# A segment softmax on one core: the scan carries the preceding edges' maximum, ScalarE clamps, VectorE scales edge rows

## The reference

```python
q = (x @ qw + qb).reshape(N, HEADS, CH)
k = (x @ kw + kb).reshape(N, HEADS, CH)
v = (x @ vw + vb).reshape(N, HEADS, CH)
alpha = jnp.sum(q[dst] * k[src], axis=-1) * SCALE
m = jax.ops.segment_max(alpha, dst, num_segments=N)
a = jnp.exp(alpha - m[dst])
denom = jax.ops.segment_sum(a, dst, num_segments=N)
a = a / denom[dst]
msg = v[src] * a[:, :, None]
out = jax.ops.segment_sum(msg, dst, num_segments=N).reshape(N, HEADS * CH)
return out + x @ sw + sb
```

## Time and profile before

| | us |
|---|---|
| median of three runs | 3342.61 |
| fastest, slowest of them | 3339.86, 3343.45 |
| the profiled execution: its span, first to last instruction | 3538.4 |
| conv 0, from the first to the last copy of source rows | 715.4 to 1208.4 |
| conv 1, the same, without the first and the last steps | 1267.5 to 1853.6 |
| TensorE, VectorE, ScalarE, GpSimd busy over the span | 2701.9, 2616.7, 2012.3, 1863.6 |

### The profile page before, as it was taken

One profiled execution on the slowest core, in us unless ns is written; L12 is line 12 of the kernel. 1 busy time (PEld: TensorE's weight loads), 2 busy tenths in 40 slices (PEclk: granted clock), 3 DMA queues, 4 the chain that ended last, 5 costly groups with the idle time before them and its releaser, 6 DMA issues. The chain is left out here.

```text
span 3538.4 us, 46258 instructions
## 1 busy us (share of the span) xinstructions
PE 2701.9 (76%) x14325; PEld 1792.3 (51%) x14325; DVE 2616.7 (74%) x3171; ACT 2012.3 (57%) x3400; POOL 1863.6 (53%) x1771
## 2 busy tenths in 40 slices
PE   7799999689999778878785789999999774332332
PEld 3466666466666545555553246666666553221221
DVE  6589999889999868888884269999999994222322
ACT  0167777556665558878784258888888782111111
POOL 4477787333333276766663654554453003666665
PEclk6699999899999989999997899999999996566655
DMA  6357666556666556666662156666666653222221
GB/s 202 100 173 222 212 221 220 189 176 197 197 202 199 160 167 207 210 207 208 197 205 74 47 159 172 188 196 193 183 194 174 183 171 107 58 64 63 74 69 39
DMA packets 474800, 573.34 MB, mean 162 GB/s; under 512 B 65347, under 2 KB 283133, under 8 KB 474431
## 3 DMA queue, kind: packets, MB, share of 16 engines
q1 hardware_dynamic: 412744, 457.19, 42.0%
q0 software_dynamic: 56480, 111.88, 11.6%
q10 hardware_dynamic: 5334, 1.32, 0.2%
HBM read 353.51 MB, written 220.55 MB: 162 GB/s over the span
## 5 line engine op out<-in xcount | busy, mean ns | idle before, releaser
L1292 POOL DMA_INDIRECT g_xd_xs<-table_x,dst_row x196 | 211.8, 1081 | 360.4 <-PE g_psT L1358 250.7
L1804 POOL DMA_INDIRECT f_xs<-table_x,src_row x196 | 192.0, 980 | 312.5 <-POOLq L1216 253.1
L775 POOL DMA_INDIRECT c_xs<-table_x,src_row x196 | 185.5, 946 | 303.9 <-PE c_psT L916 250.6
L765 POOL DMA_INDIRECT c_xs<-table_h,src_row x196 | 206.9, 1056 | 193.0 <-PE c_psT L909 94.0
L1867 ACT ACTIVATE f_reluT<-f_psY 128x512 f32<-128x512 f32 x49 | 29.3, 597 | 472.6 <-DMA table_x<-g_x3o 329.2
L497 POOL DMA_INDIRECT xs<-in_x,src_i x196 | 224.7, 1147 | 101.6 <-issue 54.0
L482 POOL DMA_INDIRECT xd<-in_x,dst_i x196 | 222.9, 1137 | 96.3 <-issue 47.9
L1811 POOL DMA_INDIRECT out<-f_xo,end_i x196 | 198.7, 1014 | 121.1 <-DVE f_xo L1904 61.6
L1292 POOL DMA_INDIRECT g_xd_xs<-table_x,src_row x196 | 218.6, 1116 | 59.8 <-issue 59.8
L765 POOL DMA_INDIRECT c_xd<-table_h,dst_row x196 | 200.8, 1025 | 59.8 <-issue 59.8
L1363 PE MATMUL g_psP<-w_center,g_turns 128*128 128x128 f32 x1568 | 197.1, 279 | 13.6 <-ACT g_turns L1492 9.1
(11 more groups left out here) (330 smaller groups left out, 8669.8 us busy)
## 6 DMA issues: line engine op xcount, KB each, us to landing
g_share<-shares SPq DMA_DIRECT2D x196, 192.0 KB
xn<-in_x SPq DMA_DIRECT2D x49, 512.0 KB
table_x<-xo SPq DMA_DIRECT2D x49, 512.0 KB
table_x1b<-xb SPq DMA_DIRECT2D x49, 512.0 KB
c_xn<-table_x SPq DMA_DIRECT2D x49, 512.0 KB
table_h<-c_xo SPq DMA_DIRECT2D x49, 512.0 KB
c_xn<-table_h SPq DMA_DIRECT2D x49, 512.0 KB
c_x1r<-table_x1b SPq DMA_DIRECT2D x49, 512.0 KB
```

Source lines behind the costliest of these rows:

```text
L765: pool.indirect_dma_start(out=quarters(rows[:, s, :])[j], out_offset=None, in_=table, in_offset=edge_index(columns, now.n, j)).then_inc(la ...
L775: pool.indirect_dma_start(out=quarters(xs[:, s, :])[j], out_offset=None, in_=table, in_offset=edge_index(h.src_row, now.n, j)).then_inc(sr ...
L1292: pool.indirect_dma_start(out=quarters(xd_xs[:, s, k, :])[j], out_offset=None, in_=table, in_offset=edge_index(columns, now.n, j)).then_in ...
L1804: pool.indirect_dma_start(out=quarters(xs[:, s, :])[j], out_offset=None, in_=table, in_offset=edge_index(h.src_row, now.n, j)).then_inc(sr ...
```

## The change

`m`, `drop`, `dropm` and `u` are gone. The scan takes the maximum first and adds `far` of the *following* edge afterwards, so that `past[e]` is the masked maximum of the edges before edge e in its segment. One subtraction `above = psA - past` stands for the three operations; ScalarE makes from it `under = relu(-above)` and `over = relu(above)`, and then `p = exp(-under)` and `c = exp(-over)`. The load of `far` is shifted by one edge, and its last column is set by a memset. In conv 1 the four edge blocks are no longer scaled on ScalarE; VectorE multiplies them by `rstd` in one operation between `num` and `kq`, and tells so by its own semaphore, for which SyncE waits before the edge store.

```diff
@@ conv, SyncE
                     if not layer:
-                        here = bass.ds(now.n * TILE, TILE)
-                        wait(sp, m_ready, now.n - 1)
-                        sp.dma_start(h.far[:, here], io["far"][:, here].to_broadcast([P, TILE])
+                        first, count = now.n * TILE, min(TILE, EDGE_ROWS - 1 - now.n * TILE)
+                        wait(sp, past_ready, now.n - 1)
+                        sp.dma_start(h.far[:, first:first + count],
+                                     io["far"][:, first + 1:first + 1 + count].to_broadcast([P, count])
                                      ).then_inc(far_landed[s], 16)
...
-                    store_group(sp, g, a, b, t, result, xo, out_ready, node_stored, edge_stored)
+                    if g and a == 0:
+                        sp.wait_ge(out_ready, g.n + 1)
+                        sp.dma_start(node_rows(result, g.n), xo[:, g.slot, 0:2, :]).then_inc(node_stored[g.slot], 16)
+                    if b == 3:
+                        e = Tile(g.i, g.c - 1)
+                        sp.wait_ge(oute_ready, e.n + 1)
+                        sp.dma_start(edge_rows(result, e.n), by_row(xo[:, g.slot, 2, :])).then_inc(edge_stored[e.slot], 16)
@@ conv, ScalarE
                 if last:
-                    act.wait_ge(dropm_ready, last.n + 1)
-                    wait(act, num_ready, last.n)
-                    nc.scalar.activation(c[:, :], dropm[:, :], ACT.Exp).then_inc(c_ready, 1)
-                    act.wait_ge(u_ready, last.n + 1)
+                    act.wait_ge(above_ready, last.n + 1)
+                    wait(act, p_ready, last.n)
+                    nc.scalar.activation(under[:, :], above[:, :], ACT.Relu, scale=-1.0).then_inc(under_ready, 1)
+                    wait(act, c_ready, last.n)
+                    nc.scalar.activation(over[:, :], above[:, :], ACT.Relu).then_inc(over_ready, 1)
+                    act.wait_ge(under_ready, last.n + 1)
                     wait(act, pv_ready, last.n)
                     wait(act, den_ready, last.n)
-                    nc.scalar.activation(p[:, :], u[:, :], ACT.Exp).then_inc(p_ready, 1)
+                    nc.scalar.activation(p[:, :], under[:, :], ACT.Exp, scale=-1.0).then_inc(p_ready, 1)
+                    act.wait_ge(over_ready, last.n + 1)
+                    wait(act, num_ready, last.n)
+                    nc.scalar.activation(c[:, :], over[:, :], ACT.Exp, scale=-1.0).then_inc(c_ready, 1)
...
                 if layer and g:
-                    scale_rows(t, g, a, b, 3, 12).then_inc(out_ready, 1)
+                    if a == 0:
+                        scale_rows(t, g, a, b, 3, 8).then_inc(out_ready, 1)
@@ conv, VectorE
-                    nc.vector.tensor_tensor_scan(m[:, s, 1:TILE + 1], h.far[:, here], psA[:, :], m[:, s, 0:1],
-                                                 ALU.add, ALU.max).then_inc(m_ready, 1)
+                    nc.vector.tensor_tensor_scan(past[:, s, 1:TILE + 1], psA[:, :], h.far[:, here], past[:, s, 0:1],
+                                                 ALU.max, ALU.add).then_inc(past_ready, 1)
...
-                    nc.vector.tensor_tensor(drop[:, :], m[:, s, 0:TILE], m[:, s, 1:TILE + 1],
-                                            ALU.subtract).then_inc(drop_ready, 1)
-                    wait(dve, p_ready, last.n)
-                    nc.vector.tensor_tensor(u[:, :], psA[:, :], m[:, s, 1:TILE + 1], ALU.subtract).then_inc(u_ready, 1)
-                    dve.wait_ge(drop_ready, last.n + 1)
-                    wait(dve, c_ready, last.n)
-                    nc.vector.scalar_tensor_tensor(out=dropm[:, :], in0=drop[:, :], scalar=0.0, in1=h.far[:, here],
-                                                   op0=ALU.min, op1=ALU.add).then_inc(dropm_ready, 1)
+                    wait(dve, over_ready, last.n)
+                    wait(dve, under_ready, last.n)
+                    nc.vector.tensor_tensor(above[:, :], psA[:, :], past[:, s, 0:TILE],
+                                            ALU.subtract).then_inc(above_ready, 1)
...
+                if layer and b == 3:
+                    e = Tile(g.i, g.c - 1)
+                    dve.wait_ge(rstd_ready, g.n + 1)
+                    wait(dve, edge_stored[e.slot], 16 * e.half)
+                    scale = rstd[:, g.slot, 8:12].rearrange("p (b o) -> p b o", o=1).to_broadcast([P, 4, P])
+                    nc.vector.tensor_tensor(by_row(xo[:, g.slot, 2, :]), by_row(pre[:, g.slot, 2, :]), scale,
+                                            ALU.mult).then_inc(oute_ready, 1)
```

More of the change, by code:

```diff
@@ L804, in conv @@
         q, kq = sb("q", [P, TILE]), sb("kq", [P, TILE])
-        m = sb("m", [P, 2, TILE + 1])
-        drop, dropm, c, u, p = (sb(n, [P, TILE]) for n in ("drop", "dropm", "c", "u", "p"))
+        past = sb("past", [P, 2, TILE + 1])
+        above, over, under, c, p = (sb(n, [P, TILE]) for n in ("above", "over", "under", "c", "p"))
         pv, den, num = sb("pv", [P, TILE]), sb("den", [P, 2, TILE]), sb("num", [P, 2, TILE])
@@ L827, in conv @@
              "starts_sp", "turned", "turned_sb", "q_ready", "q_sb", "k_ready", "v_ready", "kq_ready", "a_ready",
-             "carry_ready", "m_ready", "drop_ready", "dropm_ready", "c_ready", "u_ready", "p_ready", "pv_ready",
+             "carry_ready", "past_ready", "over_ready", "under_ready", "c_ready", "above_ready", "p_ready", "pv_ready",
              "den_ready", "num_ready", "lnd_ready", "rden_ready", "agg_ready", "en_ready", "ee_ready", "oute_ready",
@@ L949, in alike @@
                 pe.wait_ge(kq_ready, now.n + 1)
-                wait(pe, u_ready, now.n)
+                wait(pe, above_ready, now.n)
                 nc.tensor.matmul(psA[:, :], h.w["heads8"][:, :], kq[:, :], start=True, stop=True).then_inc(a_ready, 1)
@@ L1020, in scale_rows @@
                 act.wait_ge(rstd_ready, g.n + 1)
-                free_of_stores(act, t, g, a, b, node_stored, edge_stored)
+                wait(act, node_stored[g.slot], 16 * g.half)
                 for j in range(max(first, 4 * a), min(end, 4 * b)):
@@ L1094, in _ @@
         def _(dve):
-            nc.vector.memset(m[:, 0, 0:1], 0.0).then_inc(carry_ready, 1)
+            if not layer:
+                nc.vector.memset(h.far[:, EDGE_ROWS - 1:EDGE_ROWS], -FAR)
+            nc.vector.memset(past[:, 0, 0:1], -FAR).then_inc(carry_ready, 1)
             def fill_dst(e):
@@ L1140, in step @@
                 if last:
-                    dve.wait_ge(m_ready, last.n + 1)
-                    wait(dve, dropm_ready, last.n)
-                    nc.vector.tensor_tensor(drop[:, :], m[:, s, 0:TILE], m[:, s, 1:TILE + 1],
-                                            ALU.subtract).then_inc(drop_ready, 1)
-                    wait(dve, p_ready, last.n)
-                    nc.vector.tensor_tensor(u[:, :], psA[:, :], m[:, s, 1:TILE + 1], ALU.subtract).then_inc(u_ready, 1)
-                    dve.wait_ge(drop_ready, last.n + 1)
-                    wait(dve, c_ready, last.n)
-                    nc.vector.scalar_tensor_tensor(out=dropm[:, :], in0=drop[:, :], scalar=0.0, in1=h.far[:, here],
-                                                   op0=ALU.min, op1=ALU.add).then_inc(dropm_ready, 1)
-                    wait(dve, drop_ready, last.n)
-                    nc.vector.tensor_copy(m[:, 1 - s, 0:1], m[:, s, TILE:TILE + 1]).then_inc(carry_ready, 1)
+                    dve.wait_ge(past_ready, last.n + 1)
+                    wait(dve, over_ready, last.n)
+                    wait(dve, under_ready, last.n)
+                    nc.vector.tensor_tensor(above[:, :], psA[:, :], past[:, s, 0:TILE],
+                                            ALU.subtract).then_inc(above_ready, 1)
+                    wait(dve, above_ready, last.n)
+                    nc.vector.tensor_copy(past[:, 1 - s, 0:1], past[:, s, TILE:TILE + 1]).then_inc(carry_ready, 1)
                 soon = t.tile(-1)
```

4 lines of the change are left out of this document (2 added, 2 removed).

## The result

The changed kernel takes 3447.77 us, the median of four runs (3442.65 to 3458.53). The kernel before took 3342.47 us beside it (four runs, 3339.86 to 3343.45). The ratio is 1.0327, 95% interval 1.0314 to 1.0339: 105.3 us slower, where 95 were forecast. The profiled execution of the changed kernel took 3442.65 us.

What follows compares the result with a forecast made beforehand. The prediction took a ring of waits through TensorE and ScalarE, not VectorE's amount of work, to bound the kernel. Conv 0's 45 us plus conv 1's 50 made 95, added to 3342.6 for 3437 us; range 3380 to 3467 us.

Steps and rivals of the forecast that it cites:

- Rival 2: Both convolutions: VectorE sets the pace after all, so its removed work pays 86 us, giving 3256 us; chance 0.06.
- forecast 45 us: Conv 0: two relus delay the `xnT` copy 1.04 us, less 0.11 to spare, 0.93 over 48 steps; bounds 37 and 58.
- The time to spare: Conv 0: TensorE's path back to the logits product would be free 0.11 us before that product starts.
- rival 3: Conv 0: longer waits bring TensorE's granted clock to 0.94, 32 us more, giving 3469 us; chance 0.07.
- the sum's own bound of 126: Both convolutions: the upper end of the summed loss, whose bounds were 79 to 126 us.
- forecast 50 us: Conv 1: `pv` about 0.45 us later plus 0.60 edge scaling, 1.05 over 48 steps; bounds 42 and 68.
- 0.45 softmax, 0.60 scaling: Conv 1, per step: `pv` starts about 0.45 us later through `p`; edge scaling between `num` and `kq` adds 0.60.
- Rival 1: Conv 1: irregular steps averaging 12.74 us hide the longer ring of 12.43; only conv 0 pays, 3388 us; chance 0.15.
- the 195.8 us between span and median: Whole kernel before: the runs' median lies 195.8 us below the profiled span; microseconds were carried over, not the share.
- The bounds were 0.44 and 0.66: ScalarE, both convolutions: low and high price in us of one 128x512 relu, taken as 0.52.
- its ring: Conv 0 step of 10.25 us: TensorE, then ScalarE, then back by VectorE or TensorE; conv 1's undisturbed ring 11.38 us.

Runs made afterwards that it cites:

- e8: The kernel before without `drop` and `dropm` on VectorE, `c` being the exponential of `u` (part of the softmax left out): 3334.18 us, ratio 0.9992 to the kernel before.
- e6: The changed kernel with two more 128x512 subtractions on VectorE behind `above`, results unread: 3450.15 us, ratio 1.0324 to the kernel before.
- e2: The kernel before with only the edge scaling on VectorE between `num` and `kq`, old softmax: 3364.39 us, ratio 1.0084 to the kernel before.
- e4: The kernel before with the new softmax in conv 0 alone, conv 1 unchanged: 3397.32 us, ratio 1.0167 to the kernel before.
- e7: The changed kernel with a third 128x512 relu on ScalarE behind `over` in both convolutions, result unread: 3554.66 us, ratio 1.0642 to the kernel before.
- e5: The changed kernel with conv 0's relus ahead of `q` and the earlier tile's edge relu behind the first `xnT` copy: 3379.41 us, ratio 1.0121 to the kernel before.
- e9: The kernel before with the new softmax in conv 0 alone, its relus ahead of `q`, edge relu moved later: 3328.99 us, ratio 0.9973 to the kernel before.
- e11: The kernel before with `p` made ahead of `c` on ScalarE in both convolutions: 3509.31 us, ratio 0.9952 to the kernel before at 3527.89 us.
- e12: The kernel before with `p` made ahead of `c` on ScalarE in conv 0 alone: 3512.72 us, ratio 0.9962 to the kernel before at 3527.59 us.
- e1: The changed kernel with conv 1's edge rows scaled on ScalarE again, so new softmax only: 3427.44 us, ratio 1.0268 to the kernel before.
- e10: The kernel before with new softmax and early relus in conv 0, and `kq` ahead of `den` and `num` in both convolutions: 3334.00 us, ratio 0.9988 to the kernel before.
- e3: The changed kernel with VectorE's edge scaling moved from ahead of `kq` to behind `agg`: 3430.34 us, ratio 1.0287 to the kernel before.

## Why the prediction was right, and where it was off

**What bounds the kernel: right.** Work on VectorE ahead of its wait for `p` (conv 0) or for the square (conv 1) has no price (e8, e6); behind that wait it has its full price (e2: 0.62 a step). Work on ScalarE behind `q` has its full price once the spare time is used up (e4: 0.83 of 1.04; e7: 0.52 of 0.52), and ahead of `q`, in conv 0, none (e5). Rival 2 is out by e8 alone.

**Conv 0: forecast 45 us, measured 53** (544.0 against 491.0 in e2, whose conv 0 is that of the kernel before). It is two errors of opposite sign.
- The step: forecast 11.18, measured 11.08. The relu's 0.52 was right. The time to spare was 0.21, not 0.11. I had counted TensorE's path up to the logits and stopped there. But in the kernel before the logits start 1.00 after the second `own_rows` and the next transposes 0.96 after the logits; in the changed one it is 0.89 and 0.86 (1007.07 to 1007.93). Both tenths were VectorE's late `kq`. That is also why e5, e9, e11 and e12 reach 10.05: VectorE's path from `p` on did set the step of the kernel before, by 0.21, and `p` ahead of `c` takes it off. The step gives 48 x 0.83 = 40 us. The transposes that follow the logits of 1000.47 in the kernel before, and of 1007.07 in the changed one:

```profile
1001.43 0.60 PE L916 MATMUL c_psT<-w_ident,c_xs 128*128 128x128 f32 x4
```
```profile
1007.93 0.60 PE L923 MATMUL c_psT<-w_ident,c_xs 128*128 128x128 f32 x4
```

- The clock: forecast nothing. The other 13 us are the 9 falls, at up to 1.66 each. This is rival 3, to which I gave 0.07. It priced the effect at 32 us with a clock of 0.94; the clock was 0.97 over conv 0 as a whole. It did not come in place of the forecast, as I had set it up, but on top of it. The range was wide enough.

That the two errors took 5 us off each other is luck. So is the number of falls: the same instructions had 16 in e4, where conv 0 is 11 us longer. (The range's upper end, 3467, is 2 us below what the sum's own bound of 126 gives.)

**Conv 1: forecast 50 us, measured 51** (596.1 against 544.8). `pv` starts 4.62 after the copy of source rows and not 4.16, 0.46 for the forecast 0.45; the scaling is spaced 0.62 for 0.60; 11.35 + 0.46 + 0.62 = 12.43, measured 12.44. The sum over both convolutions is 104 of the 105.3 us by the medians. What the prediction lacked is the second way round by `rden`; it has no part in the changed kernel's time, but the "0.45 softmax, 0.60 scaling" do not come off singly as it says (e1 has 0.67 a step, e2 0.62, both together 1.09).

**Rival 1** (conv 1 hides its part) did not happen. Its evidence, the mean step of 12.74, was of the chip (or the hour) and not of the kernel: undisturbed, the mean is 11.35 and there is nothing to hide in. The timed runs were on chips of the other kind. The prediction named the 195.8 us between span and median, left them unexplained, and carried microseconds over all the same. That this did no harm is because the sum was made from single steps. A sum from the two profiles' lengths would give 544.0 - 493.0 + 596.1 - 620.3 = 27 us.

**The price of a relu on ScalarE.** The bounds were 0.44 and 0.66; the rows shown have 0.52 wherever two relus stand behind each other at full pace (0.54 in e5). The Trainium skill's page "ScalarE: Activation LUTs", in "What ACT_TABLE_LOAD costs", gives one element per cycle and lane for every function alike, float32 and bf16: with scale and bias as immediates 186 ns and 0.833 ns per element, with 93 ns of overlap from one to the next. For 512 elements that is an estimate of 0.52 us from the page's figures. The trace agrees, and with it the low bound need not have stood. The rule that the prediction weighed, in "Rules for kernel authors" of the same page of the Trainium skill, is relu on VectorE because it is faster there in bf16. No run here has a relu on VectorE. The float32 operations on two tiles of this size that the rows do show there take 0.60, a relu 0.52 on ScalarE. The loss came from the place, as e5 shows.

## What to carry to other kernels

Follow one step round its ring before you move work from the busiest engine: in conv 0 the 96% busy engine gave up 1.2 us a step for nothing, and a 60% busy one took on 1.04 a step and cost 53 us, 40 by the step and 13 by the clock. The same two instructions are free in the engine's wait and, but for 0.21 us to spare, cost their full length behind it, so place is worth more than count. Look for a second way round the ring too: it ate a part of what e1 was meant to gain and all of e10's. Compare the span of a profile with the median first, and if they differ trust single undisturbed steps, not means or differences of lengths.

## What was not expected of the hardware

- TensorE's clock falls in steps in which it never waits longer than 1.52 us at a stretch and is busy 83% (166.06 of 200.00 us) just before. A fall comes in some steps and not in others of the same instructions, in 9 to 16 of 48, and costs 1.66 us. In the changed kernel, e1, e3, e4 and e6 most of them come in trains, one in every second step, with a dozen or more steps without one between two trains. With waits of 2.04 (conv 0 of e7) there are 35, with 1.73 (its conv 1) 27, and with 1.21 at most (conv 1 of the changed kernel) none, though there TensorE's waits of a step add up to 2.67, more than conv 0's 1.86. What starts and ends a train is open. The timed runs of e7 lie within 0.12% of each other all the same (3551.40 to 3555.74 us).
- The same kernel has two levels of time. The kernel before takes 3337 to 3342 us (median) in four sets of runs, on at least three chips, and 3528 us in two sets on two others, where the steps of conv 1 are irregular and those of conv 0 are not. No chip of the experiments was met in a second set, so chip and hour can't be told apart.
